# Shared mixture stage of an eight-stage kernel: down products placed before the spreads, and scaling placed last on VectorE

## The reference, cut to what matters

```
shared = silu(x @ sh_up_w + sh_up_b) @ sh_down_w + sh_down_b
scores = softmax(xf @ gate_w.T)
topk_w, topk_i = top_k(scores, 2)
topk_w = topk_w / (topk_w.sum(-1) + 1e-20)
comb = (one_hot(topk_i, 8) * topk_w[..., None]).sum(axis=1)
h  = silu(einsum('nd,edh->neh', xf, up_w) + up_b)
ye = einsum('neh,ehd->ned', h, down_w) + down_b
y  = einsum('ned,ne->nd', ye, comb)
x  = x + y + shared
```

## Time and profile before

| what | value |
|---|---|
| median of 3 runs | 1106.92 us (1106.59 to 1107.39) |
| the profiled execution's own time | 1109.05 us |
| its span, first to last instruction | 1107.0 us |
| mean granted TensorE clock | 0.981 |
| busy share of the span | PE 90%, PEld 72%, DVE 71%, ACT 50%, POOL 21% |
| first `up0` of the stage to the next stage's first projection | 440.41 to 532.03 us |

### The profile page before, as it was taken

How to read it: one execution, slowest core, us unless ns; L and a number is a source line. 1 busy time by engine, 2 the same in 40 slices (tenths; PEclk the granted TensorE clock), 3 DMA queues, 4 the chain that set the end, 5 groups by cost and what they waited for, 6 DMA issues and landing times.

```text
span 1107.0 us, 33398 instructions
## 1 busy us (share of the span) xinstructions
PE 992.4 (90%) x12437; PEld 795.1 (72%) x12437; DVE 786.3 (71%) x1907; ACT 555.3 (50%) x1068; POOL 236.5 (21%) x247
## 2 busy tenths in 40 slices
PE   4789999989999997999989999888999988989887
PEld 4558888867777776777868778766778777656646
DVE  6776877587777776655496777566777667887877
ACT  2543443655555553434366565554656553445543
POOL 4651221122222221422010000000000002255300
PEclk9899999999999998999999999999999999999989
DMA  9300000000000000000000000000000000000001
GB/s 362 155 1 1 0 0 0 1 2 2 1 0 0 0 0 2 1 0 1 1 3 0 0 0 0 2 1 2 0 0 0 1 2 1 0 1 1 0 1 39
DMA packets 5926, 16.23 MB, mean 15 GB/s; under 512 B 729, under 2 KB 4962, under 8 KB 5218
## 3 DMA queue, kind: packets, MB, share of 16 engines
q1 hardware_dynamic: 5858, 15.29, 3.6%
HBM read 14.24 MB, written 1.05 MB: 14 GB/s over the span
## 4 chain that ended last, share of the span: by engine, by line
PE 61%; DVE 14%; issue 11%; DVEq 8%; ACT 3%; POOL 1%; POOLq 1%; ACTq 0%
PE banks L1852 9%; PE banks L1925 5%; PE banks L1897 5%; PE banks L1554 5%; PE banks L974 3%; PE banks L1885 3%; PE banks L1597 2%; PE banks L1913 2%; PE banks L1671 2%; PE banks L1469 2%; PE banks L1230 2%; PE banks L1637 2%; PE banks L1584 1%; PE banks L375 1%; PE banks L2387 1%
## 5 line engine op out<-in xcount | busy, mean ns | idle before, releaser
L1860 ACT ACTIVATE work<-banks 128x512 f32<-128x512 f32 x128 | 74.9, 600 | 70.8 <-PE banks L1852 70.8
L364 POOL TENSOR_TENSOR rstd<-var,nhalf 128x2 f32<-128x2 f32 x64 | 44.9, 702 | 297.1 <-DVE var L335 289.2
L1450 ACT ACTIVATE work<-work 128x1024 f32<-128x1024 f32 x64 | 67.9, 1060 | 43.3 <-DVEq L1446 25.8
L1852 PE MATMUL banks<-xT_all,weights 128*128 (+1 forms) x384 | 86.2, 380 | 2.3 <-ACT work L1974 1.6
L2008 DVE TENSOR_TENSOR work<-banks,neg_mask 128x512 f32<-128x512 f32 x64 | 40.9, 685 | 63.4 <-PE banks L1885 62.2
L1852 PEld LDWEIGHTS banks<-xT_all,weights 128*128 128x128 f32 x384 | 71.6, 190 | 13.7 <-ACT work L1974 2.4
L1012 ACT ACTIVATE work<-banks,weights 128x256 f32<-128x256 f32 x128 | 53.5, 472 | 54.6 <-PE banks L964 53.7
L1476 ACT ACTIVATE work<-banks 128x512 f32<-128x512 f32 x128 | 68.2, 604 | 12.0 <-PE banks L1469 7.7
L1925 PEld LDWEIGHTS banks<-weights,work 128*128 128x128 f32 x512 | 58.4, 191 | 15.0 <-ACT work L1974 15.0
L974 PE MATMUL banks<-weights,work 128*128 128x128 f32 x512 | 63.1, 276 | 5.4 <-DVE work L1121 5.0
L974 PEld LDWEIGHTS banks<-weights,work 128*128 128x128 f32 x512 | 60.9, 191 | 9.6 <-ACT work L1012 8.2
(11 more groups left out here) (349 smaller groups left out, 2291.5 us busy)
## 6 DMA issues: line engine op xcount, KB each, us to landing
weights<-wpack SPq DMA_DIRECT2D x1, 5381.5 KB, 32.2
weights<-wpack SPq DMA_DIRECT2D x1, 2060.0 KB, 12.6
weights<-wpack SPq DMA_DIRECT2D x1, 2049.0 KB, 16.9
weights<-wpack SPq DMA_DIRECT2D x1, 1160.5 KB, 19.2
x_all<-x_in SPq DMA_DIRECT2D x2, 512.0 KB, 4.7
ctxT_all<-ctxT_in SPq DMA_DIRECT2D x1, 1024.0 KB, 6.7
out<-x_all SPq DMA_DIRECT2D x8, 128.0 KB, 1.8
rows<-rows_in SPq DMA_DIRECT2D x1, 832.0 KB
```

Source lines behind the costliest of these rows:

```text
L1450: act.activation(sm[:, u, :], sm[:, u, :], ACT.Exp, scale=scale).then_inc(h["exp"].sem, 1)
L1852: ins = pe.matmul(bank(ring.bank(f"qk{c}"))[:, j * PT:(j + 1) * PT], wt[:, 2 * (c % 4) + j, :], cols(src, p), start=True, stop=True)
L1860: act.activation(dst.rearrange("p c t -> p (c t)"), bank(ring.bank(f"qk{c}")), ACT.Copy) \
```

## The change

On TensorE, the down products of pair p-1 are issued right behind `up4` of pair p, ahead of the wait for `combT` and ahead of the spreads. Before, they stood behind the spreads. On VectorE, `scale` of pair p moves from the place behind `sum_up` to the end of the part, behind `weigh` and `ending`. Since `weigh` of pair p+1 now overwrites `comb4` ahead of the scaling of pair p, it gets a wait of its own until the transposes of pair p have read it. The router's drain is kept. The number of arithmetic instructions is the same on every engine.

```diff
--- before.py
+++ after.py
@@ -1247,6 +1247,10 @@
                     ins.then_inc(banks_filled, 1)
                     up(ring, i, p, 3)
                     up(ring, i, p, 4)
+                    if loop:
+                        down(p - 1, 1 - k, ring.emptied_before(i, "b3"))
+                    elif p:
+                        down(p - 1, 1 - k, s.body.emptied(p - 1, "b3"))
                     pe.wait_ge(*ring.emptied(i, "combT"))
                     for g in range(4):
                         settle(pe)
@@ -1259,10 +1263,6 @@
                                             tile_position=(32 * g, 0))
                             if e:
                                 ins.then_inc(banks_filled, 1)
-                    if loop:
-                        down(p - 1, 1 - k, ring.emptied_before(i, "b3"))
-                    elif p:
-                        down(p - 1, 1 - k, s.body.emptied(p - 1, "b3"))
                     if loop or p > 1:
                         turn_normed(pe, g_of(s, p) - 1)
                     elif p == 0:
@@ -1362,11 +1362,12 @@
                         sort(ring, i, p + 1)
                     if late:
                         sum_up(p - 2)
-                    scale(ring, i, k)
                     if ring is s.body:
+                        v.wait_ge(banks_filled, ring.filled(i, "combT"))
                         weigh(p + 1)
                     if late:
                         ending(p - 2)
+                    scale(ring, i, k)
 
                 def head():
                     v.memset(small[:, 128:384], 0.0)
```

## The result

The changed kernel takes 1115.0 us in the median (1113.38 to 1118.34, 5 runs), and the kernel before 1106.92 in the same session. The ratio is 1.008, with a 95% interval of 1.0058 to 1.0102. So it is about 8 us slower, where 6.3 were forecast. The profiled execution took 1118.34 us with a span of 1116.5. Its busy shares hardly moved against the earlier trace rows. TensorE's busy time rose by 8.6 us for the same number of instructions, so part of its work ran more slowly. Not all of that is the change's: 390.26 - 385.36 = 4.9 us of it lie ahead of the stage, where the two kernels are the same.

The account below looks back on a forecast made before the run. TensorE, busy 90% of the span, was taken to bound the kernel. Losses of 3.1 + 2.4 + 2.4 less gains of 3.3 gave 4.6 us, plus 1.7 for one clock drop: 6.3 us slower, 1113.2 us, range 1109.6 to 1116.6.

Parts of the forecast that it names:

- Loss at pairs 0 and 1: TensorE's router of pair 2 waits for VectorE's late scaling of pair 0 and starts 3.1 us late; 3.1 us lost.
- Losses at the general waits: Ahead of pair 7 and the next stage's first projection, TensorE waits for the scaling; 2.4 us lost at each.
- The rival that they cost nothing: At the two general waits, TensorE would soon stand idle anyway; no slower, -0.2 us, 1106.7 us; chance 0.10.
- Gains in the loop: Pairs 2 to 5: TensorE's gaps ahead of spreads and transposes go; 0.65 us a pair, 2.6 us in four.
- 0.67 - 0.12 - 0.17: Per loop pair: 0.67 us gained from `up3` to spreads, less 0.12 for later transposes and 0.17 for register waits.
- The bubble of 0.17 behind the down products: In the loop, the spreads' four register waits show behind short down products as 0.17 us of idle time.
- One bound of the gains: All gains together, in the loop and pairs 6 and 7, with all small costs at zero: near 4.2 us.
- The rival in which the gaps ahead of the spreads stay: In the loop, register waits show as 0.54 us; gains 1.8 us, not 3.3; 1114.7 us with one drop; chance 0.12.
- Gain in pair 7: From `up3` to the spreads 0.44 us goes, less 0.12 and 0.09: 0.2 us gained.
- The clock: One drop of TensorE's clock behind the long idle stretch, none behind the two short ones; 1.7 us lost.
- The rival with two drops: Two or three clock drops behind the new idle stretches: 4.6 + 3.4 or 5.1, 1114.9 to 1116.6 us; chance 0.20.
- The main case: Whole kernel: 4.6 us of losses less gains, plus one clock drop of 1.7; 6.3 us slower, 1113.2 us.

Follow-up runs that it names:

- e6: The changed kernel, with unread products on TensorE filling its waits at the router of pair 2 and behind pairs 6 and 7: 1105.96 us, ratio 1.0017.
- e1: The changed kernel, but VectorE scales pair 0 ahead of `weigh`, as before: 1107.16 us, ratio 1.0023.
- e7: The kernel before, with VectorE's new order alone and TensorE's order as before: 1108.17 us, ratio 1.0028.
- e2: The changed kernel, but TensorE keeps the order of before in pairs 6 and 7: 1106.78 us, ratio 1.0017.
- e4: The changed kernel with pair 0 scaled first on VectorE, and TensorE's two general waits replaced by waits for each bank: 1103.42 us, ratio 0.9996.
- e10: The changed kernel, with unread products on TensorE only ahead of the two general waits: 1110.42 us, ratio 1.0039.
- e9: The changed kernel, with unread products on TensorE only ahead of the router of pair 2: 1108.21 us, ratio 1.0019.
- e5: The changed kernel once more, unaltered, on another chip, against the kernel before: 1113.30 us, ratio 1.0077.

## Why the prediction was right, and where its size was off

**Loss at pairs 0 and 1: right.** Forecast 3.1 us late at the router. It stood idle for 3.10 us and started 4.13 us behind `up0` where it had been 0.87 (447.43 to 448.30), so 3.3 late, by the mechanism named (GpSimd's power, `weigh`, the first scaling). From the first spreads to the next `up0` it is 12.86 us before and 463.55 - 447.45 = 16.10 in `e6`, whose clock is full: 3.2 us against a forecast of 3.1. `e1` and `e7` show that it hangs on the order on VectorE alone. (In the working, 449.19 + 1.52 is 450.71 and not 450.74, which changes nothing.)

**Losses at the general waits: right.** Forecast 2.33 of idle time, 2.4 with the signal; measured 2.31 and 2.42. `e2` hides them with the down products, and `e4` takes them away at the wait. The rival that they cost nothing fell.

**Gains in the loop: the sum right, its parts not.** Forecast 0.65 us a pair. From `up0` of pair 2 to `up0` of pair 7 the time fell from 62.34 us to 61.53 in `e6`, with 2.48 of new waiting inside, so the gains there are 3.3 us against a forecast of 3.1. But I gave 0.67 - 0.12 - 0.17 = 0.38 of a pair to TensorE's part and 0.27 to VectorE's. A pair takes 11.97 us with VectorE's part alone (`e7`) and 489.82 - 478.04 = 11.78 with both, so TensorE's part is worth only 0.2. The bubble of 0.17 behind the down products is only half there: the spreads follow 2.20 us after the second half began, 0.08 over the 2.12 of plain work. But `up3` to the down products takes 1.40 us (483.19 to 484.59), where I had 1.30, and the down products behind them are slower too. I read both as the price of changing the tiling mode, for which the sum of the loop had only 0.12. The down products' two halves start 487.62 - 484.59 = 3.03 us apart behind up products, and 474.55 - 471.62 = 2.93 behind the spreads in `e7`. VectorE's part gave more than its 0.27, because what stands between the transposes and the next `up0` shrank as well once TensorE no longer waited ahead of them. Register and branch work stands there, which I take to be now covered. From the transposes to `up0` it takes 0.27 us behind pair 3 now (490.90 to 491.17). Before, it took 0.77 behind pair 3 (483.48 to 484.25), as the timeline's row shows:

```profile
484.25 1.13 PE L1230 MATMUL banks<-xT_all,weights 128*128 x4 [0.33 <-issue]
```

That is the end of a loop round. Behind the other pairs it was 0.35 or 0.36 before, and is 0.27 or 0.28 after and 0.22 in `e7`.

One bound of the gains was summed wrongly. With all the small costs at zero they would be 3.3 + 4 x 0.29 + 2 x 0.21 = 4.9 and not 4.2, so the low end of the sum was 3.0 and not 3.7 us. The stated range still holds it (1106.92 + 3.0 = 1109.9).

The rival in which the gaps ahead of the spreads stay fell as well, since no spreads in the loop waited.

**Gain in pair 7: wrong, and small.** Forecast 0.2 us. From `up0` of pair 7 to the next stage it is 10.75 us before and 13.44 in `e6`, 2.7 more with 2.64 us of waiting, so nothing came back.

**The clock: the term that was mis-sized.** The step "I take one drop, behind the long stretch, and none behind the two short ones" failed, and so did its price of 1.7 us. The waits less the gains came out at 5.1 us for a forecast of 4.6. The drops cost 4.5 us in the stage, for which I had put 1.7. There were two in the stage of the changed kernel, in both of its profiles. And the one behind the long wait cost 2.8 us by `e10`, since the low level lasted longer (in the changed kernel three rows of 2 us at 0.50, and a part of a fourth), where the drop from which I took the price had ended after two. The rival with two drops named the right number, at too low a price. That its 1114.9 us lies next to the measured 1115.0 is in part luck: it puts 8.0 us on the stage, where the profile has 9.6. The main case came out 1.8 us low on the median, inside the range, which the rivals had widened to that side. The stretch of 2.42 us without a drop was no ground for excluding one behind 2.31 us. The Trainium skill, "TensorE: Matmul & The Clock Gate", Part 1, says that the number of slow matmuls behind a cold start varies between runs of one kernel. These traces agree: a like wait was followed by none (after, the third), two (after, the second) or three windows of low clock (`e9`, the second). Behind the long wait it hardly varied: in all five profiles in which it wasn't filled (after, `e2`, `e5`, `e7`, `e10`) the clock dropped, and the cost was 2.8 to 3.0 us in the four where the spreads give it.

The stage's 101.24 - 91.62 = 9.6 us in the profile are thus 3.2 + 2.5 + 2.7 = 8.4 us of waits, less 3.3 of gains, plus 4.5 of clock. The signal behind each wait is counted with it. The median difference of 8.1 us is smaller than the stage's. The profiled execution was the slowest of the five, and with the stage of `e5`, 100.94 us, the difference is 9.3.

## What to carry to other kernels

When work that covered a wait is moved, look first at the ends of the loop: the first pair, whose inputs come late, and the last ones, where a general wait asks for everything. The loop alone would have shown a clean gain of about 3 us. Price each new idle stretch of TensorE like these, of 2.3 to 3.1 us, with its length and a drop of the clock on top: here that was nothing to 3 us for the shorter ones and about 3 us each time for the long one. Where it can't be avoided, fill it: unread products cost no time and gave 4.2 to 4.5 us of the stage back. And compare the stage as well as the whole kernel, since the clock also drops in stages that no edit touches, and not equally often.

## What the runs showed of the hardware

- A wait of 3.10 or 3.11 us was followed by a clock of 0.50 in five profiles of five. One of 2.30 or 2.31 us was as well (after, `e1`, `e5`, `e9`), and waits of 2.42 us in the same kernel and elsewhere were not, though in another kernel (`e9`) one of 2.42 was. Among the shorter ones the length of the stretch alone doesn't decide.
- Products that nobody reads, put into such a wait, kept the clock at 1.00 wherever they stood (`e6`, `e9`, `e10`), and the next real product started as late as without them.
- The low level lasted from one and a half to over three rows of 2 us. What ended it isn't shown.
- From the transposes at the end of a loop round to the next `up0` TensorE took 0.77 us where the transposes had waited (before), and 0.27 (after) or 0.22 (`e7`) where they had not. That this is register and branch work, hidden in the second case, is my reading of the rows.
- Idle time without a named releaser varied between 20.4 (`e6`) and 27.1 us (`e5`) over the kernels here, mostly in stages that no experiment touched, and the part behind the stage between 564.2 (`e6`) and 575.0 us (before), with the clock low at none to four places in it. Either is more than the loop's whole gain. This is why a change of 3 us was judged by its stage and by the ratio together.
